# Five engine programs with their loop over 24 pairs of graphs written out as straight code

## The reference

```python
qk = X @ Wqk; q, k = jnp.split(qk, 2, axis=-1); v = X @ Wv          # layer 0
agg = jnp.einsum('bij,bjd->bid', adj, k * mask[:, :, None])
w = inv_scale * mask * jnp.einsum('bid,bid->bi', q, agg)
x = _layernorm(x + jax.nn.softmax(w, axis=1)[:, :, None] * v)
...
weight = adj * jnp.exp(jnp.einsum('bqd,bkd->bqk', query, keyt))     # layer 1
weight = weight / jnp.sum(weight, axis=2, keepdims=True)
x = _layernorm(x + jnp.einsum('bqk,bkd->bqd', weight, value))
```

## Time and profile before

| | |
|---|---|
| median of 3 runs | 305.0 us (304.91 to 305.19) |
| profiled execution | 305.39 us |
| its span, first to last instruction | 303.6 us |
| TensorE (PE) matmul busy | 294.1 us |
| VectorE (DVE) busy | 230.0 us |
| ScalarE (ACT) busy | 214.2 us |
| GpSimd (POOL) busy | 197.6 us |
| granted TensorE clock, mean | 0.994 |

### The profile page before, as it was taken

How to read it: one execution, slowest core, us unless ns; L and a number is a source line. 1 busy time by engine, 2 the same in 40 slices (tenths; PEclk the granted TensorE clock), 3 DMA queues, 4 the chain that set the end, 5 groups by cost and what they waited for, 6 DMA issues and landing times.

```text
span 303.6 us, 6841 instructions
## 1 busy us (share of the span) xinstructions
PE 294.1 (97%) x1956; PEld 269.6 (89%) x1956; DVE 230.0 (76%) x698; ACT 214.2 (71%) x509; POOL 197.6 (65%) x237
## 2 busy tenths in 40 slices
PE   8998999999999999999999999999999999999991
PEld 7788999999999999999999999999999999999980
DVE  1478778877777887777788777778877777887684
ACT  3455667778777777877777787777778777776753
POOL 2447766667876666687666668766666876664431
PEclk9999999999999999999999999999999999999997
DMA  7930233332344432233443223434322344210012
GB/s 231 331 79 36 87 90 122 88 91 85 105 122 121 121 102 86 71 104 121 121 121 108 79 75 101 121 121 121 109 86 72 96 121 121 87 54 36 35 37 104
DMA packets 19165, 31.26 MB, mean 103 GB/s; under 512 B 2128, under 2 KB 6608, under 8 KB 19152
## 3 DMA queue, kind: packets, MB, share of 16 engines
q1 hardware_dynamic: 19152, 31.11, 33.2%
HBM read 22.71 MB, written 8.39 MB: 102 GB/s over the span
## 4 chain that ended last, share of the span: by engine, by line
PE 93%; DVE 3%; issue 2%; ACT 1%; POOL 1%; POOLq 0%; DVEq 0%
PE ps L820 22%; PE ps L822 22%; PE ps L821 21%; PE ps L928 8%; PE ps L923 8%; PE ps L905 4%; PE ps L1034 1%; PE ps L880 1%; PE ps L874 1%; PE ps L843 1%; PE ps L1039 1%; DVE x L615 1%; PE ps L885 1%; DVE stats L577 0%; DVE x L623 0%
## 5 line engine op out<-in xcount | busy, mean ns | idle before, releaser
L356 POOL TENSOR_TENSOR rstd<-var_eps,minus_half 128x4 f32<-128x4 f32 x31 | 31.6, 1018 | 72.4 <-DVE var_eps L740 72.4
L432 ACT ACTIVATE x<-x_sum,shift,rstd 128x256 f32<-128x256 f32 x60 | 32.9, 595 | 59.3 <-POOL shift L359 59.3
L820 PE MATMUL ps<-w_hi,xt_hi 128*128 128x512 f32 x128 | 57.2, 447 | 0.5 <-DVE w_lo L806 0.5
L822 PE MATMUL ps<-w_hi,xt_lo 128*128 128x512 f32 x128 | 50.4, 394 | 0.0
L821 PE MATMUL ps<-w_lo,xt_hi 128*128 128x512 f32 x128 | 50.3, 393 | 0.0
L285 POOL TENSOR_TENSOR x1b<-x,bv_all 128x512 f32<-128x512 f32 x32 | 41.4, 1293 | 7.0 <-DVE x L615 3.3
L366 POOL TENSOR_TENSOR xt_lo<-xt_raw,xt_hi 128x512 fp32r<-128x512 f32 x31 | 39.9, 1286 | 3.9 <-ACT xt_hi L414 3.9
L343 POOL TENSOR_TENSOR x_lo<-x_raw,x_hi 128x512 fp32r<-128x512 f32 x28 | 36.2, 1292 | 3.4 <-ACT x_hi L421 2.1
L820 PE MATMUL ps<-wv_hi,x1t_hi 128*128 128x258 f32 x124 | 37.9, 306 | 0.0
L822 PE MATMUL ps<-wv_hi,x1t_lo 128*128 128x258 f32 x124 | 35.3, 285 | 0.0
L821 PE MATMUL ps<-wv_lo,x1t_hi 128*128 128x258 f32 x124 | 35.1, 283 | 0.0
(11 more groups left out here) (140 smaller groups left out, 790.7 us busy)
## 6 DMA issues: line engine op xcount, KB each, us to landing
xt_raw<-xt_pairs SPq DMA_DIRECT2D x32, 256.0 KB, 2.7
x_raw<-x_pairs SPq DMA_DIRECT2D x32, 256.0 KB, 3.1
out_pairs<-x SPq DMA_DIRECT2D x31, 256.0 KB, 2.7
adjt<-adjt_pairs SPq DMA_DIRECT2D x32, 129.0 KB, 2.0
p<-params SPq DMA_DIRECT2D x1, 770.0 KB, 6.9
p<-params SPq DMA_DIRECT2D x1, 512.0 KB, 3.9
p<-params SPq DMA_DIRECT2D x1, 256.0 KB, 4.8
out_pairs<-x SPq DMA_DIRECT2D x2, 128.0 KB, 1.8
```

The source lines that it names most:

```text
L356: nc.gpsimd.tensor_tensor(rstd[r % 2][:, :, :], var_eps[:, :, :], minus_half[:, :, :], ALU.pow)\
L432: last = nc.scalar.activation(out[:, graph(g)], in_[:, graph(g)], ACT.Identity, bias=shift[r % 2][:, layer, g:g + 1], scale=rstd[r % 2][:, ...
L820: nc.tensor.matmul(out, s_hi, m_hi, start=first, stop=False)
L822: return nc.tensor.matmul(out, s_lo, m_hi, start=False, stop=last)
```

## The change

The loop and its constants are taken out, and `slots` calls `slot(t, t)` for all t with a Python number. All waits compare with constants, and all DMA addresses are constants. No operation on data, no buffer, no wait and no order of operations is changed on any engine.

```diff
-LOOP_FROM, LOOP_TO, UNROLL = 4, 28, 4
...
-    return not isinstance(pair, int) or 0 <= pair < PAIRS
+    return 0 <= pair < PAIRS
...
-        def slots(eng, slot, first=FIRST):
+        def slots(slot, first=FIRST):
 
-            for t in range(first, LOOP_FROM):
-                slot(t, t)
-            with eng.Fori(LOOP_FROM, LOOP_TO - UNROLL + 1, UNROLL) as base:
-                for j in range(UNROLL):
-                    slot(base + j, LOOP_FROM + j)
-            for t in range(LOOP_TO, DRAIN + 1):
+            for t in range(first, DRAIN + 1):
                 slot(t, t)
```

More of the change, by code:

```diff
@@ L257, in _ @@
                 sp.sem_inc(q, 16)
-            slots(sp, slot)
+            slots(slot)
             for u in range(DRAIN - 2, PAIRS - 1):
@@ L403, in _ @@
             mask_adj(0, 0)
-            slots(pool, slot)
+            slots(slot)
             drain()
@@ L559, in _ @@
             nc.scalar.activation(w0_hi[:, 1, 0:DIM], m0_ps[:, 1, :], ACT.Copy, scale=ATT_SCALE).then_inc(m0_hi_done, 1)
-            slots(act, slot)
+            slots(slot)
             drain()
@@ L813, in _ @@
             dve.wait_ge(consts_ready, 1)
-            slots(dve, slot)
+            slots(slot)
             drain()
@@ L1059, in _ @@
             transpose_next(-1, -1)
-            slots(pe, slot, 0)
+            slots(slot, 0)
             drain()
```

## The result

The kernel after takes 305.63 us (median of 22 runs, 304.60 to 307.90) where the kernel before takes 305.00 (22 runs, 304.43 to 305.45). The ratio is 1.0029, with a 95% interval of 1.0018 to 1.0040. It is slower by 0.6 us, where 0.9 us less was forecast, and its runs spread over 3.3 us instead of 1.0.

What follows compares the result with a forecast made beforehand. TensorE's matmuls were taken to bound the kernel at 8.80 us per slot. The loop's excess, 194.51 - 193.60 = 0.91 us, goes and all else counts nothing: 305.0 - 0.9 = 304.1 us, range 303.7 to 304.8.

Steps and rivals of the forecast that it cites:

- What bounds the kernel: Whole kernel: TensorE, busy 294.1 of 303.6 us; its matmuls alone fit in 8.80 us per slot, loop slots averaged 8.841.
- branches and register instructions: Loop slots: five branches back cost 0.59 us, VectorE's branch being what counts; register instructions cost 0.02 per slot, 0.32 us.
- the sum: The 22-slot loop stretch: 194.51 - 193.60 = 0.91 us go, kept as 0.9.
- Rival B: Loop slots: only the branches pay and slots stay at 8.82; gain 0.49 us, to 304.5; chance 0.18.
- rival D: Slot boundary: another wait just behind keeps the branch's time from coming back; nothing changes, 305.0 us; chance 0.04.
- Instruction supply: Queue 8: 16 packets, 10 more than now, each 0.9 to 1.5 us of one DMA engine; cost to TensorE taken as nothing.
- rival C: Every second slot from slot 6: late instructions stall TensorE, up to 10 x 1.5 = 15 us, giving 319; chance 0.07.
- The transfers start by the same semaphores as before, so nothing new collides: DMA transfers: even if the engines' waiting cover were gone, they would only be faster and nothing new collides; cost nothing.
- The cover I named for GpSimd: GpSimd waits 72.4 us in all for VectorE's variance, so what it saves becomes a longer wait; counted at nothing.

Runs made afterwards that it cites:

- e2: Kernel before with only TensorE's program kept in the loop, the other four engines straight; 304.65 us, ratio 0.9990.
- e3: Kernel before with only TensorE's program straight, the other four engines kept in the loop; 306.77 us, ratio 1.0057.
- e9: e1 with the fifth adjacency buffer placed behind all other tiles, so every old tile keeps its address; 304.46 us, ratio 0.9985.
- e8: e2 with e1's edit (five adjacency buffers, loads one slot earlier); 303.64 us, ratio 0.9954.
- e11: Kernel after, unchanged, run again as a control on the same chip as e9 and e10; 305.92 us, ratio 1.0038.
- e10: e1 with 4 more VectorE instructions (waits) in its prologue; 303.33 us, ratio 0.9949.
- e1: Kernel after with five adjacency buffers in place of four and each adjacency load issued one slot earlier; 303.27 us, ratio 0.9948.
- e7: e1 with 6 more VectorE instructions (waits) in its prologue; 303.77 us, ratio 0.9956.
- e5: Kernel after with an unused fifth adjacency buffer of 1,032 bytes a partition, loads and waits unchanged; 304.79 us, ratio 0.9991.
- e6: Kernel before, with its loop, plus the same unused buffer as e5; 303.99 us, ratio 0.9971.

## Why the prediction was wrong

**What bounds the kernel; branches and register instructions: right.** The loop's excess went, and a little more: 1.10 us, where the sum had 0.9 (28 x 8.80 was forecast, and the undisturbed slots took 8.793). The 8.91 did not come from TensorE's branch (e2), and the chain puts it on VectorE's (rows 6, and e3). Two readings were wrong, at no cost to the forecast. TensorE's own branch does cost something. The 0.14 at the branch was held against the 0.15 of slot 4, but TensorE enters the loop there. In straight code before it the same matmul takes 0.12, in the trace of before:

```profile
46.39 0.12 PE ps L820
```

In e2 it is 0.16 at a branch, and the slots at the branches and at the loop's entry are 8.83 to 8.84. They are all that TensorE's loop costs, 0.2 us in e2 (246.79 against 246.62 in e9); e8 gives 0.3. And the 0.02 of an ordinary slot is not the price of TensorE's register instructions by themselves, since those slots are 8.79 in e2 and 8.75 in e8. Whose it is, is open. Rival B is out, rival D too.

**Instruction supply: the number right, the price wrong.** "I take nothing, because the lower rows are of the same kind of fetch in the same kind of code." This is the step that failed. The 16 packets came as forecast. The 0.9 to 1.5 us are the time of a packet (0.93 to 1.47 us in the trace of before); that it is one DMA engine's is not shown, since the traces name the queue of a packet and not its engine. I asked only whether TensorE starves behind a packet, which is rival C too, and it never did: e9 has all 16 packets and no late engine but for VectorE's 0.35. The cost went to the data. The four packets in the trace of before that met an adjacency load came 0.0 to 0.3 us after its issue and held up nothing. The later ones, which had drifted to 0.9 us and more, that trace could not show. But it did show that a packet slows the load: those four landed in 2.2 to 3.0 us, the other 24 in 2.0 to 2.1. The slowest of them, issued at 268.68 us, and its use:

```profile
adjt<-adjt_pairs SPq DMA_DIRECT2D x1, 129.0 KB, 3.0
...
271.94 0.61 POOL L277 TENSOR_TENSOR adjm<-adjt 128x256 f32<-128x256 f32 x1
```

It landed 0.2 us before GpSimd took it. To read the slots alone, all of 8.80, was to miss this. In the profiled execution of the kernel after, the late tiles cost 1.5 us; between the medians of e11 and e9 it is 1.5 as well.

**"The transfers start by the same semaphores as before, so nothing new collides": wrong.** The instruction packets are themselves new transfers. The cover I named for GpSimd, 72.4 us of waiting for the variance, was in the wrong place of its slot. It lies ahead of line 350 (356 before); from the mask to `adjm_lo` GpSimd had no slack at all, since 0.75 us there became 0.76 us on TensorE (18.34 us for two slots of 8.79). The load's own slack was visible in the trace of before: 3.1 to 3.3 us from issue to use, for a landing of 2.0 and up to 3.0.

**Not thought of: VectorE's crossing.** Its straight program comes in packets too, on queue 14 (17 in the whole span, 7 before). One of its crossings falls on the copy and the sum, the very link that I had found to be tight (1.14 against 1.18 us), and costs 0.35 us. Other crossings cost nothing that can be read: TensorE's slots with a packet and no late tile are 8.79, and VectorE's crossings show in one slot alone. In e10 one in the drain shows too (0.49 us of idle time against 0.13). The cost I priced at nothing for TensorE had to be asked of VectorE as well.

**Sum.** -1.10 for the loop, +0.35 for the crossing, +1.53 for late tiles is +0.78 us in slots 1 to 28 of the profiled execution (248.08 against 247.30), and the start was 0.18 earlier, so the span grew by 0.6. The chance of slower was put at 0.08, and the only rival behind it was another, C, so the cause that made it slower had no share in that chance.

## What to carry to other kernels

Code written out straight is fetched while it runs (here 16 packets on queue 8, and 6 with the loop), and its packets slow the transfers of data that they meet (here from 2.0 to as much as 4.0 us for 129 KB). Before unrolling, look for loads that are used soon after they are issued, and give them a step of lead (here 1,032 bytes a partition): the version with lead (e1) beats both kernels, 303.27 us, but about 1 us of that belongs to a chance of the layout. The lead without it (e9) gives 304.46, 0.3 us less than before on that chip. And when a wait is tight, ask of both ends of it which instructions stand between, a branch (here 0.09 to 0.15 us) or a block boundary (0.35) among them.

## What the hardware showed that was not expected

- A block crossing cost VectorE 0.35 to 0.39 us where nothing hid it (idle 0.46, 0.49 and 0.49 us, where it is 0.11, 0.10 and 0.13 otherwise). The instructions held up are its 192nd (e7), 576th (e1 and the kernel after) and 960th (e10), steps of three times 128; queue 14 moved 0.14 MB in 17 packets.
- Queue 8 moved 0.26 MB in 16 packets, one every two slots. The loop's body of four slots, two packets long by that beat, ran six times with no packet between 90 and 262 us.
- On TensorE, 40 more wait instructions on a semaphore that was otherwise reached after 1.0 us set the first matmul back by 5.3 - 1.0 = 4.3 us, about 0.1 us each.
- An unused tile of 1,032 bytes a partition ahead of others shortened TensorE's slots from 8.79 to 8.75 us (e1, e5), and was worth 1.0 us with the loop (e6). The cause is open.
- A packet that came 0.5 to 1.3 us after the load's issue made it land in 3.0 to 4.0 us instead of 2.0; one within 0.5 us of the issue, in 2.2 to 3.1. Why is open.
